# Audio tower, 1 core: convolution with its band moving, centring put into attention's weights, w1 loaded once, and a new order of steps

## What is computed

```python
# token stage: two dense tanh layers, a square, two dense tanh layers, convolution of 15 taps, stride 2
out = tanh(tanh(x @ W_in[0] + b_in[0]) @ W_in[1] + b_in[1])
out = abs(core_diag) * out * out
out = tanh(tanh(out @ W_out[1] + b_out[1]) @ W_out[0] + b_out[0])
h = depthwise_conv(pad(out, 7), conv_filter, stride=2)          # (8, 375, 64)
# attention without softmax
n = layernorm(h)
q, k, v = n @ Wq.T, n @ Wk.T, n @ Wv.T
a = relu(where(upper triangle, 0, q @ k.T)) / max(row, 1)
h = h + (a @ v) @ Wo.T
# mixture of 16 experts, top 2
n = layernorm(h)
w, idx = softmax(top_k(n @ gate_w + gate_b, 2))
moe = sum over the two of w * (relu(n @ w1[e] + b1[e]) @ w2[e] + b2[e])
h = h + layernorm(n + moe) * gamma + beta
```

## Time and profile before

| | us |
|---|---|
| median of 3 runs | 189.54 (185.79 to 190.82) |
| the profiled execution's own time | 186.72 |
| its span | 184.8 |
| TensorE busy | 159.4 |
| DVE busy | 104.9 |
| ACT busy | 92.9 |
| POOL busy | 29.7 |

### The profile page before, as it was taken

How to read it: one execution, slowest core, us unless ns; L and a number is a source line. 1 busy time by engine, 2 the same in 40 slices (tenths; PEclk the granted TensorE clock), 3 DMA queues, 4 the chain that set the end, 5 groups by cost and what they waited for, 6 DMA issues and landing times.

```text
span 184.8 us, 4222 instructions
## 1 busy us (share of the span) xinstructions
PE 159.4 (86%) x1594; PEld 91.9 (50%) x1594; DVE 104.9 (57%) x422; ACT 92.9 (50%) x149; POOL 29.7 (16%) x46
## 2 busy tenths in 40 slices
PE   5999999597695999999979999999999949979710
PEld 5887677255683465434544535455444424446310
DVE  0322632296769879853676885439896246172132
ACT  0356669164434645555466556654556534636410
POOL 8960020021303212000032000001400002000030
PEclk9999999969999999999999999999999999999995
DMA  3556478400000791004985005795000699320001
GB/s 96 116 88 166 126 191 178 83 0 2 4 0 15 218 253 38 4 10 94 243 220 122 5 10 138 209 238 141 0 5 10 173 227 248 75 45 0 0 0 42
DMA packets 16111, 17.72 MB, mean 96 GB/s; under 512 B 8421, under 2 KB 12353, under 8 KB 15964
## 3 DMA queue, kind: packets, MB, share of 16 engines
q1 hardware_dynamic: 14928, 16.74, 35.9%
q10 hardware_dynamic: 844, 0.64, 1.1%
q0 software_dynamic: 320, 0.09, 1.1%
HBM read 16.49 MB, written 0.97 MB: 94 GB/s over the span
## 4 chain that ended last, share of the span: by engine, by line
PE 42%; issue 15%; SPq 13%; DVE 12%; DMA 10%; POOL 4%; ACT 1%; POOLq 1%; DVEq 0%
PE z L1052 13%; PE y L1066 12%; DMA w_last<-last_row 6%; SPq L398 5%; PE a L992 4%; DMA gate_all<-gates_dram 3%; POOL stat_A L581 3%; PE a L982 2%; DVE h L758 2%; SPq L326 2%; SPq L367 2%; PE a L1013 1%; PE z L1028 1%; DVE halves_A L630 1%; PE a L998 1%
## 5 line engine op out<-in xcount | busy, mean ns | idle before, releaser
L528 ACT ACTIVATE hid<-z 128x750 f32<-128x750 f32 x64 | 50.8, 797 | 36.3 <-PE z L1052 29.1
L1052 PE MATMUL z<-xg,w_s 64*64 64x375 f32 x512 | 55.0, 479 | 1.6 <-DVE xg L850 1.6
L1066 PE MATMUL y<-hid,w_s 64*64 64x375 f32 x512 | 53.5, 480 | 0.7 <-ACT xg L438 0.4
L850 DVE TENSOR_TENSOR xg<-xa_t,gate_all 128x375 f32<-128x375 f32 x60 | 31.9, 546 | 20.9 <-PE z L1052 11.8
L1052 PEld LDWEIGHTS z<-xg,w_s 64*64 64x64 f32 x512 | 20.3, 132 | 20.5 <-issue 14.5
L1066 PEld LDWEIGHTS y<-hid,w_s 64*64 64x64 f32 x512 | 19.4, 132 | 19.7 <-issue 11.3
L581 POOL TENSOR_TENSOR stat_A<-stat_A,minus_half 125x6 f32<-125x6 f32 x4 | 6.2, 1561 | 57.1 <-DVE stat_A L763 57.1
L581 POOL TENSOR_TENSOR stat_F<-stat_F,minus_half 125x6 f32<-125x6 f32 x4 | 5.8, 1440 | 51.5 <-DVE stat_F L640 51.5
L587 POOL TENSOR_TENSOR stat_t<-stat_t,minus_half 125x6 f32<-125x6 f32 x4 | 6.4, 1598 | 40.9 <-DVE stat_t L729 40.9
L863 PE MATMUL a<-ident 128*128 128x128 f32 x56 | 10.2, 344 | 1.6 <-POOL ident L543 1.6
L863 PEld LDWEIGHTS a<-ident 128*128 128x128 f32 x56 | 8.9, 245 | 2.7 <-POOL ident L543 1.6
(11 more groups left out here) (163 smaller groups left out, 205.0 us busy)
## 6 DMA issues: line engine op xcount, KB each, us to landing
gate_all<-gates_dram SPq DMA_DIRECT2D x54, 187.5 KB, 4.1
gate_all<-gates_dram SPq DMA_DIRECT2D x12, 93.8 KB, 2.8
w_s<-in_L_ffn_w_dram SPq DMA_DIRECT2D x2, 504.0 KB
w_last<-last_row SPq DMA_DIRECT2D x2, 504.0 KB
x_in<-in_x_dram SPq DMA_DIRECT2D x4, 187.5 KB
out_dram<-y_out SPq DMA_DIRECT2D x7, 93.8 KB
w_s<-in_L_ffn_w_dram SPq DMA_DIRECT2D x1, 512.0 KB, 12.9
x_in<-in_x_dram SPq DMA_DIRECT2D x3, 168.0 KB
```

Source lines behind the costliest of these rows:

```text
L528: act.activation(hid[:, n % HID], z_pair[e % 2][:, :, 0:TO], ACT.Relu).then_inc(hid_ready.sem, 1)
L850: nc.vector.tensor_tensor(xg[:, n % XG], xa_t[g % 2][:], gate_all[:, e], ALU.mult).then_inc(xg_ready.sem, 1)
L1052: ins = mm(z[e % 2][b][q, 0:TO], w1_s[f, e, q], xg[f, n % XG], start=True, stop=True)
L1066: ins = mm(y[h][b * D:(b + 1) * D, 0:TO], w2_s[q, e, :], hid[q, (E * g + e) % HID, b], start=e == 0, stop=e == E - 1)
```

## The change

- The convolution (T.5) has the tokens' features stationary and the band moving: six matmuls a group, whose moving parts are 122, 125, 70, 128, 70 and 66 columns. Its result comes with the features on partitions; ACT evicts it as `ut`. A new step T.6 transposes it back (L970 of the changed kernel), and ACT evicts that as `hres`. Group 0 uses other banks for it.
- Attention reads `ut` for queries and keys, and `hres` for the values. Instead of centring the rows, each of Wq, Wk and Wv has its mean taken away (`w_mid`, new DVE step S.4). DVE's centring of T.6, the transposes A.0 and their eviction are gone.
- w1, b1 and the broadcast last row are loaded for 64 partitions only; after DVE's subtraction SP copies the four pieces to the other 64 partitions (new SP steps S.10 to S.13).
- x of groups 1 to 3 is loaded so that a transposed block holds its tokens in order: three runs of 512 bytes a row instead of one of 1536, without `cuts`, and the evictions are contiguous.
- The filter's padded row and the band are smaller; ACT issues the band's load after another step, and its table load earlier.
- Step F.4 is split: the scaling stays F.4, the output is F.6.
- All lists of steps are new. On SP, F0.5 and F1.5 (stores) now stand ahead of A2.12 and A3.12. 22 filler matmuls instead of 28.

```diff
+        PAD = TAPS // 2
+        first = [max(0, (TOK * c - PAD + 1) // 2) for c in range(NT)] + [TO]
+        stop = [min(TO, (TOK * (c + 1) - 1 + PAD) // 2 + 1) for c in range(NT)]
+        for m in range(NR):
+            stop[2 * m] = first[2 * m + 2]
+        lead = [max(TOK * m - first[2 * m + k] for m in range(NR)) for k in range(2)]
+        SPAN = max(stop[2 * m + k] - TOK * m + lead[k] for m in range(NR) for k in range(2))
+        MID = 2 * TOK
+        tops = [MID + PAD + TOK * k + 2 * lead[k] for k in range(2)]
+        BANDW = max(tops) + 1
+        assert BANDW + TOK <= ROW and min(tops) >= 2 * SPAN
...
-                T0.0 S0.8 W0.6 T0.1 W0.3 T0.2 W0.2 T1.0 W0.7 T0.3 T1.1 S0.1 T0.4 S0.2 T1.2 T0.5 T2.0 T1.3 T2.1 W0.5
...
+                T0.0 W0.4 S0.8 T0.1 W0.2 T0.2 W0.5 T0.3 W0.4 T0.4 S0.1 W0.2 T0.5 S0.2 T1.0 T0.6 A0.1 T2.0 T3.0 A0.2
...
-                A0.12 A1.12 A2.12 F0.5 A3.12 F1.5 F2.5 F3.5""",
+                S0.10 S0.11 S0.12 S0.13 A0.12 A1.12 F0.5 A2.12 F1.5 A3.12 F2.5 F3.5""",
...
+                src = x[PAIR * g + b].rearrange("(c p s) d -> p c s d", c=NR, s=2)
+                for p0, p1 in zip(cuts, cuts[1:]):
+                    dst = x_in[g][p0:p1, b].rearrange("p (c s) d -> p c s d", s=2)
+                    eng.dma_start(dst, src[p0:p1]).then_inc(x_in_ready[g], 32 // (len(cuts) - 1))
+                return
...
+            def setup(_, s):
+                sp.wait_ge(w1_ready, s - 9)
+                es = slice(PIECE * (s - 10), PIECE * (s - 9))
+                sp.dma_start(w1_s[D:P, es], w1_s[0:D, es]).then_inc(ld_copy[s - 10], 16)
...
+            sp.dma_start(last_row[:], w1[:, DX, :]).then_inc(ld_row, 16)
             for b in range(PAIR):
-                load_x(sp, 1, b, (0, SPLIT, TOK))
+                load_x(sp, 1, b)
+            for i, w in enumerate((wq, wk, wv)):
+                sp.dma_start(w_in3[:, i, :], w).then_inc(ld_attn, 16)
             sp.dma_start(wo_s[:], wo).then_inc(ld_turn, 16)
-            sp.dma_start(wq_s[:, 0, :], wq).then_inc(ld_attn, 16)
-            sp.dma_start(wv_s[:, 0, :], wv).then_inc(ld_attn, 16)
-            sp.dma_start(wk_s[:], wk).then_inc(ld_attn, 16)
             for g in (2, 3):
                 for b in range(PAIR):
                     load_x(sp, g, b)
-            sp.dma_start(last_row[:], w1[:, DX, :]).then_inc(ld_row, 16)
-            for b in range(PAIR):
-                at, last = slice(b * D, b * D + DX), slice(b * D + DX, (b + 1) * D)
-                sp.dma_start(w1_s[at], w1[:, 0:DX, :].rearrange("e h f -> h e f")).then_inc(ld_w1, 16)
-                sp.dma_start(w1_s[last].rearrange("h e f -> h (e f)"), b1.rearrange("e f -> (e f)").unsqueeze(0)).then_inc(ld_w1, 16)
-            sp.wait_ge(w1_blank, 1)
             sp.wait_ge(ld_row, 16)
-            for b in range(PAIR):
-                sp.dma_start(w1_last[b * D:b * D + DX].rearrange("h e f -> h (e f)"),
-                             last_row[:].rearrange("e f -> (e f)").partition_broadcast(DX)).then_inc(ld_w1, 16)
+            sp.dma_start(w1_last[:].rearrange("h e f -> h (e f)"),
+                         last_row[:].rearrange("e f -> (e f)").partition_broadcast(DX)).then_inc(ld_w1, 16)
+            sp.dma_start(w1_s[DX:D].rearrange("h e f -> h (e f)"), b1.rearrange("e f -> (e f)").unsqueeze(0)).then_inc(ld_b1, 16)
+            sp.dma_start(w1_s[0:DX], w1[:, 0:DX, :].rearrange("e h f -> h e f")).then_inc(ld_w1, 16)
             sp.dma_start(w2_s[:], w2.rearrange("e f h -> f e h")).then_inc(ld_w2, 16)
...
+                elif s == 3:
+                    act.dma_start(bias_last[:, 0, :], b_out[0].partition_broadcast(TOK)).then_inc(ld_bias, 16)
+                    act.wait_ge(ld_filt, 48)
+                    shifts = bass.AP(filt_pad, 0, [[1, TOK], [1, BANDW]])
+                    act.dma_start(band[:, 0:BANDW], shifts).then_inc(ld_band, 16)
...
-                    act.copy(buf_a_g[:, 0:T].rearrange("q (b p c) -> q b c p", b=PAIR, c=NR),
-                             pair_of(g)[:, :, 0:HT].rearrange("q b (c p) -> q b c p", p=TOK)).then_inc(xt_ready.sem, 2)
+                    act.copy(buf_a_g[:, 0:T].rearrange("q (b i) -> q b i", b=PAIR), pair_of(g)[:, :, 0:HT]).then_inc(xt_ready.sem, 2)
...
+                elif s == 4:
+                    dve.wait_ge(ld_attn, 48)
+                    nc.vector.tensor_reduce(w_sum[:], w_in3[:], AX.X, ALU.add).then_inc(mid_ready, 1)
+                    dve.wait_ge(mid_ready, 1)
+                    nc.vector.scalar_tensor_tensor(out=w_mid[:], in0=w_sum[:].unsqueeze(2).broadcast_to([D, 3, D]),
+                                                   scalar=-1.0 / D, in1=w_in3[:], op0=ALU.mult, op1=ALU.add).then_inc(mid_ready, 1)
...
                     dve.wait_ge(ld_band, 16)
-                    for k in range(4):
-                        nc.vector.tensor_copy(conv_w[:, k, :], conv_block(k)).then_inc(conv_w_ready, 1)
+                    for k in range(2):
+                        nc.vector.tensor_copy(conv_w[:, k, :], band[:, tops[k]:tops[k] - 2 * SPAN:-2]).then_inc(conv_w_ready, 1)
...
+                        dve.wait_ge(ld_w1, 32)
+                        dve.wait_ge(ld_b1, 16)
+                    nc.vector.tensor_tensor(w1_s[0:DX, es], w1_s[0:DX, es], w1_last[:, es], ALU.subtract).then_inc(w1_ready, 1)
 
...
-                    src = hres[g][:]
-                    if g == 0:
-                        dve.wait_ge(conv_done.sem, conv_done.after(g, 1))
-                        src = banks_of(g)[0][0:TOK, 0:NJ * D].rearrange("p (j d) -> p j d", d=D)
-                    else:
-                        dve.wait_ge(hres_ready.sem, hres_ready.after(g, 1))
-                    moments("T", g, src)
-                    nc.vector.tensor_tensor(xc1[g][:], src, wide(mean_var["T"][:, :, 0]), ALU.subtract)\
-                        .then_inc(ln_cent["T"].sem, 1)
+                    dve.wait_ge(hres_ready.sem, hres_ready.after(g, 1))
+                    moments("T", g, hres[g])
...
                     dve.wait_ge(inv_var.sem, inv_var.after(g, 1))
-                    nc.vector.tensor_tensor(xv1[g][:], xc1[g][:], wide(stat_t[g][:, 3, :]), ALU.mult).then_inc(ln_done["T"].sem, 1)
+                    nc.vector.tensor_tensor(xv1[g][:], hres[g][:], wide(stat_t[g][:, 3, :]), ALU.mult).then_inc(ln_done["T"].sem, 1)
...
-                        mm(a1[r, 0:D], wq_s[:, 0, :], wk_s[:], start=True, stop=True)
-                        ins = mm(a1[r, 128:128 + D], wv_s[:, 0, :], wo_t[:], start=True, stop=True)
+                        mm(a1[r, 0:D], w_mid[:, 0, :], w_mid[:, 1, :], start=True, stop=True)
+                        ins = mm(a1[r, 128:128 + D], w_mid[:, 2, :], wo_t[:], start=True, stop=True)
                     ins.then_inc(prod_done, 1)
...
-                        if r < 2:
-                            pe.wait_ge(tanh4.sem, tanh4.after(g, r + 1))
-                        cs = [c for c in range(2 * r - 1, 2 * r + 3) if 0 <= c < NT]
-                        for c in cs:
-                            ins = mm(banks[0][0:TOK, r * P:(r + 1) * P], conv_w[:, c - 2 * r + 1, :], by_tile(buf_b[g])[:, c, :],
-                                     start=c == cs[0], stop=c == cs[-1])
+                        pe.wait_ge(conv_w_ready, 2)
+                    for c in (0, 2, 1, 4, 3, 5):
+                        if c in (0, 4):
+                            pe.wait_ge(tanh4.sem, tanh4.after(g, 1 + c // NR))
+                        at = first[c] - TOK * (c // 2) + lead[c % 2]
+                        ins = mm(conv_banks(g)[0][:, first[c]:stop[c]], by_tile(buf_b[g])[:, c, :],
+                                 conv_w[:, c % 2, at:at + stop[c] - first[c]], start=c == 0, stop=c == NT - 1)
                     ins.then_inc(conv_done.sem, 1)
-
-            def stage_a(g, s):
...
-                    pe.wait_ge(xn1t_ready.sem, xn1t_ready.after(g, 1))
-                    mm(a0[:, 0:TO], w_qk[:], xn1_t[:], start=True, stop=True).then_inc(q_done.sem, 1)
+                    pe.wait_ge(ut_ready.sem, ut_ready.after(g, 1))
+                    for r in range(NR):
+                        ins = nc.tensor.transpose(conv_banks(g)[1][0:TOK, r * P:(r + 1) * P], ut[g][:, r * TOK:(r + 1) * TOK], ident[:])
+                    ins.then_inc(h_turned.sem, 1)
```

158 lines of the change are left out of this document (73 added, 85 removed).

## The result

The changed kernel took 173.48 us (median of 4 runs, 172.97 to 176.59) beside 188.18 us for the kernel before: a ratio of 0.9318, 95% interval 0.9235 to 0.9401. Some executions of either kernel run longer at a lower granted clock; the ratios leave these out, while medians and ranges hold them all, so the two need not agree. Measured again on another chip it took 174.24 us, ratio 0.9282 (0.9220 to 0.9344). The forecast was 173.5 us and faster. The time is right; that it is exact is luck, since two misses nearly cancel, as the landmarks show.

The account below looks back on a forecast made before the run. TensorE's queue bounds the kernel, and until 60 us a latency chain through w1's load. Span 184.8 - 15.0 (head) + 1.0 (w1) - 0.8 (transposes) = 170.0; 171.9 with 1.9 around it; given as 173.5 for the median, range 170 to 177.

Parts of the forecast that it names:

- (1) Third product: Head, group 0's third product on TensorE: fewer fillers ahead, start at about 12.3 us instead of 14.64, 2.3 us earlier.
- (2) Convolution: Head, group 0's convolution: only tanh waited for, six matmuls in 1.3 us, result at about 17.6 instead of 21.5.
- (3) Convolution to logits: Head, convolution to first logits: 4.2 us instead of 7.8, logits at 21.8, 7.5 us earlier.
- the clock as a rival: Rival: late x or w1 in the head lowers TensorE's clock and cancels the gain, 187 us; chance 0.05.
- (4) to (7): Head, logits to first expert product: context at 26.2, h at 29.8, gates' transpose at 42.5, expert product at 45.0 us.
- Transfers: Loads: w1 lands at 27.4 against 27.1 wanted, 1.0 us charged; group 3's x there at about 19, wanted at 21.
- After 60 us: Experts and later attention: fewer transposes save 0.8 us; waits 5.9 us, much as before, so no gain booked.
- what I had named as right: Signs: logits 22 to 23, context 1.4 us near 27, h 30 to 31, experts near 46, clock 1.00, subtraction wait under 2.
- what I had named as wrong: Signs: TensorE idle for group 2 or 3's x, subtraction after 30 us, experts after 50, or later waits over 9 us.
- w1 still decides: Rival: w1 lands as late as before, so h waits 8.5 us instead of 1; 182 us, chance 0.12.
- later stages give back: Rival: denser order brings 2 or 3 more waits of 1.5 us at h and group 3's gates; 178.5 us, chance 0.17.
- Slower: Rival: TensorE waits for group 3's x, 15 us late, ahead of the first logits; 192 us, chance 0.05.

Follow-up runs that it names:

- experiment 9: Changed kernel with attention's weight loads ahead of group 1's x and all x loads cut in 112 and 13 rows, no added fillers: 169.19 us, ratio 0.9060.
- experiment 2: Changed kernel with nine more filler matmuls where TensorE was idle before the convolution: 172.59 us, ratio 0.9011.
- experiment 5: The changed kernel as it is, measured again on the second chip: 174.24 us, ratio 0.9282.
- experiment 7: Changed kernel with the stores of groups 0 and 1 put back behind the gates of groups 2 and 3 on SP: 178.49 us, ratio 0.9424.
- experiment 8: Changed kernel with w1 and its broadcast last row loaded for both partition halves again: 183.40 us, ratio 0.9733.
- experiment 3: Changed kernel with only group 1's x loads cut into 112 and 13 rows: 173.49 us, ratio 0.9048.
- experiment 6: Changed kernel with attention's weights ahead of group 1's x, all x loads cut in 112 and 13 rows, nine more fillers: 170.39 us, ratio 0.9082.
- experiment 12: Kernel before with SP's stores of groups 0 and 1 ahead of the gates of groups 2 and 3: 188.31 us, ratio 1.0034.
- experiment 1: Changed kernel with attention's four weight loads issued ahead of group 1's two x loads: 177.86 us, no ratio.
- 11: Kernel before with w1, b1 and the broadcast last row loaded for 64 partitions and copied to the others: 185.11 us, ratio 0.9844.

## Why the prediction was right, and where it wasn't

*(1) Third product:* 11.51 against 12.3; better. *(2) Convolution:* at full clock 1.52 us, not 1.3, so 0.7 us saved per group and not 0.9. My own bounds were 1.0 and, at 0.2 for each of six, 1.2; even the 1.3 that I took above both was too little. It started at 18.12, not 16.3: this step took only tanh to be waited for, and that is the first error. Tanh itself stood behind DVE's bias, and the bias behind the copy of the band and the mean of the weights, which waited for the band and Wv. Neither load was in my sum of transfers, though SP issues the weights behind group 1's x; in experiment 9, with them first, the convolution starts at 15.67.

*(3) Convolution to logits:* 5.5 us forecast (the pieces behind the convolution add up to 4.0, not to the 4.2 that I wrote), 8.1 in the profile, 5.27 in experiment 9. The steps were right, the clock not: 2.8 us are 0.50 against 1.00. I had the clock as a rival at 0.05, with "no gap over 1 us between 10 and 37 us". There was one of 1.60, and behind it and the 0.80 that follows the clock fell; with the first filled up it didn't (experiment 2). So this rival came true in a fifth of its size; the two errors, 1.8 and 2.8 us, make up the 4.4 us by which the logits miss, less 0.2 of shorter steps.

*(4) to (7):* logits to context 4.4 forecast, 4.51 found; context to h 3.6 and 3.98; h to the gates' transpose 12.7 and 12.74; from there to the first expert product 2.5 and 2.29. In experiment 9, where TensorE hardly waits, the whole chain ends at 44.47 against 45.0. The method, durations of rows laid along the new order, was sound. Where loads are late it says nothing.

*Transfers.* The charge of 1.0 us for w1 was not paid in the changed kernel, and yet its landing was mis-sized: 31.3 us in experiments 2 and 5, 29.8 in 7, not 27.4. The mistake is upstream. Group 3's x was still awaited at 22.6 to 23.6 us (experiments 2, 7 and 8), against 19 in the forecast. The DMA queue of SP, from 7 to 11 and from 15 to 21 us (packets, MB, share of 16 engines):

```profile
q1 hardware_dynamic: 713, 0.34, 30.3%
...
q1 hardware_dynamic: 1292, 0.68, 40.4%
```

From 15 to 21 us it moves 215 packets per us, just what 31 ns on 6.6 engines gives. But from 7 to 11 it moves only 178, and in between, from 11 to 15, only 94: the attention weights, the band and POOL's loads moved there (experiment 3), all of which I had left out. At 215 packets per us those two stretches would have held 630 packets more, 2.9 us of the 3.9 by which w1 is late; that is an estimate from these rows. My 6.6 engines were no clean reading either: q1's share in the kernel before is 35.8% from 20 to 22 us and 52.1% from 22 to 23, and the earlier trace rows averages the two. The estimate by the rule in the Trainium skill, "DMA: Bandwidth & Descriptors", section "Why a DMA increments its semaphore by 16 and not by 1", was 22 for group 3's x, closer than my 19. By the same rule a load of 112 rows runs on 16 engines, and the runs agree: with all loads cut, the DMA engines' busy share rose from 0.36 to 0.81, the twelve were issued in 5.95 us and nothing waited for x (experiment 6). With the head as forecast, w1 at 31.3 would have cost about 4 us instead of 1; experiment 2 shows this. Two delays lay beside each other, and the later one hid the other.

*After 60 us.* I booked -0.8 and no gain from the waits. The second chip's run has 111.8 against 114.1 us, 2 us better than booked; both long waits went. The profiled run of the result doesn't show it, since its clock was 0.91 from 140 to 160 us. I had described both mechanisms and dared no number. Experiment 7 shows that the stores' place is worth some 2.7 us here, experiment 12 that it is worth nothing in the old order.

*The sum.* Against the profiled execution before, the forecast was 171.9; the comparable run on the second chip took 174.29. So the sum was 2.4 us short: 4.4 us at the first expert product (50.45 against 46.0), 2 given back behind it. The 1.6 us that I added for the median of before hid most of this, which is luck.

*The signs.* Of what I had named as right, only the first subtraction's wait of under 2 us and the context product's 1.49 us came. Logits, context, h and the first expert product are 3 to 5 us behind it, and the clock was not 1.00. Of what I had named as wrong, the subtraction stood after 30 us (30.24 and 31.31), the experts started after 50 in experiment 5, and TensorE waited for group 3's x in experiments 2, 7 and 8. By these signs the head was mispriced, though the time came out.

*Rivals.* "w1 still decides" and "later stages give back" didn't happen; experiment 8 shows how near the first was. "Slower" had the right place and a price far too high: the waits for x add up to 4.7 us at most (0.26, 1.74 and 2.71 us in experiment 1).

**What the change consists of.** Of 13.5 us (the ratio of experiment 5), w1 loaded once carries 8.5 if it is the last part to be added (experiment 8) and 3 if it is the first (11); the stores 2.7 and 0. The parts don't add up, since each removes one of several limits that lie side by side. What the new convolution and the centring in weights are worth alone was not tried; the shorter way from convolution to logits (5.3 instead of 10.2 us) is theirs and the new order's together.

## What to carry to other kernels

List every load that a step of the chain waits for, the small ones too, with the place where it is issued and what is queued ahead of it; and look for steps that stand in an engine's list behind one that waits for a load. A chain of compute durations alone came out within 1 us, and nearly all of the error was in loads and in the clock behind them. Before pricing a part alone, ask which limit lies right beside it: a late load can hide another late load. And count a wait of over 1 us on TensorE as one that can cost twice, once as idle and once as slow work behind it.

## What was unexpected of the hardware

- Behind waits of 1.60 and 0.80 us TensorE's clock was 0.50 for all of 20 to 25 us; in experiment 7 waits of 1.78 and 0.62 us at the same place did not bring it down (convolution 1.52 us). Late in the run it is the same: 1.37 and 0.82 us at 139 to 141 us were followed by 0.50 from 142 to 144, one of 1.53 us in experiment 9 by 1.00. So near this length it can go either way. The Trainium skill, "TensorE: Matmul & The Clock Gate", section "HAM oscillation", has the clock fall in loops with waits; single waits sufficed here.
- The band is loaded from ACT's own queue, and was late all the same while SP's queue moved group 1's x: there at 15.23, and at 12.57 when only that x load was cut. Single executions vary by up to 2.3 us, but the two kinds don't overlap: 14.34 to 15.23 in five with that load uncut and ahead, 11.37 to 13.67 in five with it cut or behind the weights. A load in one queue delayed what another queue issued; whether it is the few engines that do it was not separated.
